# Post-norm decoder layer on one core: the splitting of the expert weights moved among steps 36 to 62

## What is computed

```python
x = _layernorm(x + _L0_attn_ref(x, ...))                    # state-space mixer: chunked scan, 4 heads of 64
x = _layernorm(x + _L0_xattn_ref(x, ctx_1024, ctx_1024, ...))  # cross attention: 16 heads of 8, 256 x 256 softmax
x = _layernorm(x + _L0_ffn_ref(x, ...))                     # 8 experts, the best 2 of each row
...
# experts (w0, w1: 8 x 128 x 512; wo: 8 x 512 x 128)
layer_1 = _gmm(sorted_hidden, w0, onehot)
layer_2 = _gmm(sorted_hidden, w1, onehot)
intermediate = jax.nn.silu(layer_1) * layer_2
layer_3 = _gmm(intermediate, wo, onehot)
```

## Time and profile before

| | |
|---|---|
| median of 3 runs | 422.5 us (418.44, 422.5, 1061.15) |
| the profiled execution | 415.8 us, its span 414.5 us |
| TensorE busy, granted clock | 349.5 us (84%), 0.98 of full speed |
| VectorE busy | 292.3 us (71%) |
| ScalarE busy | 235.2 us (57%) |
| GpSimd busy | 230.4 us (56%) |

### The profile page before, as it was taken

One profiled execution on the slowest core, in us unless ns is written; L12 is line 12 of the kernel. 1 busy time (PEld: TensorE's weight loads), 2 busy tenths in 40 slices (PEclk: granted clock), 3 DMA queues, 4 the chain that ended last, 5 costly groups with the idle time before them and its releaser, 6 DMA issues.

```text
span 414.5 us, 9020 instructions
## 1 busy us (share of the span) xinstructions
PE 349.5 (84%) x2869; PEld 238.0 (57%) x2869; DVE 292.3 (71%) x836; ACT 235.2 (57%) x460; POOL 230.4 (56%) x341
## 2 busy tenths in 40 slices
PE   1999977888988999988878899988997999999900
PEld 1666645556544545444444445567776899898800
DVE  3555645888788888878796736376776877877737
ACT  2677644432667666455577687744644665666514
POOL 2660598855354435271569788546575445445525
PEclk9999999999999999999999999999999999999975
DMA  8933322636515040322624343211112211111054
GB/s 269 336 110 106 87 85 77 187 94 186 171 33 166 5 140 5 99 70 75 196 69 131 117 155 102 74 32 40 53 41 78 78 53 40 53 52 35 32 171 146
DMA packets 44461, 41.97 MB, mean 101 GB/s; under 512 B 4560, under 2 KB 38416, under 8 KB 44416
## 3 DMA queue, kind: packets, MB, share of 16 engines
q1 hardware_dynamic: 41136, 35.10, 28.1%
q0 software_dynamic: 2272, 4.69, 3.2%
q10 hardware_dynamic: 1008, 1.61, 1.1%
HBM read 26.36 MB, written 14.75 MB: 99 GB/s over the span
## 4 chain that ended last, share of the span: by engine, by line
PE 56%; DVE 20%; issue 7%; POOL 7%; ACT 4%; another core or an unknown queue 3%; DMA 2%; ACTq 0%; DVEq 0%; POOLq 0%
PE banks L1017 12%; DVE nm L1210 8%; PE banks L1044 6%; PE banks L1032 4%; PE banks L859 4%; PE banks L698 4%; PE banks L907 3%; PE banks L1045 2%; PE banks L755 2%; PE banks L937 2%; PE banks L763 2%; DVE ctx_in L1152 2%; PE banks L806 2%; PE banks L934 1%
## 5 line engine op out<-in xcount | busy, mean ns | idle before, releaser
L1210 DVE TENSOR_REDUCE nm<-banks 128x4 f32<-128x1024 f32 x64 | 78.1, 1220 | 17.5 <-PE banks L850 11.4
L1520 ACT ACTIVATE probs_all<-banks 128x1024 f32<-128x1024 f32 x64 | 65.4, 1023 | 36.0 <-PE banks L859 29.6
L1017 PE MATMUL banks<-w_split,scores_in 128*128 x234 | 64.5, 410 | 0.0
L1342 DVE TENSOR_TENSOR ctx_in<-ctx_in,banks 128x512 f32<-128x512 f32 x39 | 26.8, 687 | 27.3 <-ACT ctx_in L1567 21.4
L1017 PEld LDWEIGHTS banks<-w_split,scores_in 128*128 128x128 f32 x234 | 40.8, 189 | 7.7 <-issue 0.9
L1705 POOL DMA_INDIRECT slots_dram<-rows,place_u x32 | 31.9, 996 | 23.5 <-DVE count L1302 16.1
L1727 POOL DMA_INDIRECT y_dram<-x,scatter_u x39 | 38.5, 987 | 11.4 <-POOL x L1723 9.7
L1567 ACT ACTIVATE ctx_in<-banks 128x512 f32<-128x512 f32 x39 | 23.3, 599 | 36.7 <-PE banks L1017 31.9
L859 PE MATMUL banks<-scores_in 32*128 32x256 f32 x256 | 32.2, 326 | 12.0 <-ACT probs_all L1520 6.0
L1044 PE MATMUL banks<-w_split,scores_in 128*128 x156 | 39.1, 327 | 2.8 <-ACT scores_in L1573 2.1
L907 PE MATMUL banks<-probs_all,vals 128*9 128x256 f32 x512 | 39.7, 381 | 0.2
(11 more groups left out here) (230 smaller groups left out, 802.2 us busy)
## 6 DMA issues: line engine op xcount, KB each, us to landing
scores_in<-k_dram SPq DMA_DIRECT2D x32, 128.0 KB, 2.7
scores_in<-q_dram SPq DMA_DIRECT2D x32, 128.0 KB, 2.7
ctx_in<-in_L_ffn_w SPq DMA_DIRECT2D x16, 256.0 KB, 2.7
cs_wide<-cs_dram SPq DMA_DIRECT2D x14, 256.0 KB, 3.7
scores_in<-slots_dram SPq DMA_DIRECT2D x39, 65.0 KB, 1.9
k_dram<-split_qk SPq DMA_DIRECT2D x8, 256.0 KB, 2.5
q_dram<-split_qk SPq DMA_DIRECT2D x8, 256.0 KB, 2.3
ctx_in<-in_L_ffn_wo SPq DMA_DIRECT2D x8, 256.0 KB, 2.9
```

The source lines that it names most:

```text
L1017: m = TE.matmul(up_bank(i, j), xT[:, i % XT, xh, :], all_weights[:, c + j * FF:][:, bass.ds(expert_at[i], FF)], start=n == 0, stop=n == 2)
L1210: V.tensor_reduce(most, maxima_of(n).rearrange("p (j k q) -> p j k q", j=2, k=TPS), AX_X, ALU.max, negate=True).then_inc(s["nmax"], 1)
L1520: C.activation(probs(n).rearrange("p j k q -> p (j k q)"), EXPS, ACT.Exp, scale=SCALE).then_inc(s["probs"], 1)
```

## The change

One line of constants is new, and three lines of `middle_order` use it:

```diff
 LAST_MIXER = tile_step(NT - 1) + LAGS[0][1]
+WEIGHTS_FROM, WEIGHTS_OMITTED = LAST_MIXER + 2, (40, 41, 49)
...
-        if n == LAST_MIXER + 4:
+        if n == WEIGHTS_FROM:
             for i in range(W_RING):
                 yield "load_weights", i
-        elif n >= LAST_MIXER + 6 and piece < PIECES:
+        elif n >= WEIGHTS_FROM + 2 and n not in WEIGHTS_OMITTED and piece < PIECES:
             yield "split_weights", piece
             if W_RING <= piece + 2 < PIECES:
                 yield "load_weights", piece + 2
```

## The result

The changed kernel takes 421.11 us in the median of 20 runs (419.2 to 428.43), the kernel before 419.72 us over 20 runs on the same chip. The ratio is 1.0039, with a 95% interval of 1.0022 to 1.0057: slower by 0.9 to 2.4 us, far inside 2%. Ratios here leave out executions more than 1.5% above the fastest of their kernel, while medians in us are over all executions. The sum in the prediction was +0.6 us, and the loss of the medians, 1.4 us, is over twice that. The time of 421.11 us is 1.6 us above the forecast 419.5 us and inside the range of 415 to 424 us. The profiled execution took 420.03 us (span 418.6) against 415.8 us (span 414.5).

What follows compares the result with a forecast made beforehand. A TensorE-ScalarE cycle was taken to set the pace in steps 33 to 51, TensorE from 52. +0.52 - 0.28 + 0.35 = +0.6 us on a mean of 418.9 gave 419.5 us, range 415 to 424 us.

Steps and rivals of the forecast that it cites:

- (a): Steps 36 to 38: the split put into step 37 delays ScalarE's next exponential and the delay is carried on, +0.52 us.
- (b): Steps 41 and 49: gains of the omitted splits are lost in waits tied to GpSimd's scatters; 0, bounds 0 and -0.52 each.
- the omissions pay: Rival: the waits of steps 43 and 51 aren't tied to the scatters, gains are kept; sum -0.45 us, chance 0.25.
- (c): Step 44: piece 6's load comes earlier, so its 0.42 us wait for weights goes; -0.28 us.
- (d): Steps 50 to 61: the same splits one step later, with TensorE the bound and exponentials having time to spare; 0.
- (e): Step 62, tail: the last piece on GpSimd holds VectorE's normalization, delaying TensorE's transposes; +0.35 us, bounds 0 and 0.6.
- The collision: Rival, step 43: GpSimd's piece 5 starts before VectorE's `chosen` and holds it; 0.7 to 2.0 us let through, chance 0.15.

Runs made afterwards that it cites:

- set A: Batches on one chip where the kernel before takes 418.6 to 420.0 us and ScalarE waits in step 43.
- set B: Batches on one chip where the kernel before takes 411.8 us and the wait in step 43 is absent.
- choice_first: The changed kernel, but GpSimd's piece 5 waits until VectorE's `chosen` is done; 421.53 us, 1.0028 of before.
- scatter_late_again: The kernel before with GpSimd's scatters of one tile moved from step 40 to step 44, on set A; 423.92 us in one run.
- last_ahead: The changed kernel, but the last piece is split at the start of step 62, ahead of the variance; 422.26 us, 1.0055 of before.
- after_again: The changed kernel itself, unedited, on set B; 411.63 us, 0.9995 of before.
- before_again: The kernel before, unedited, for a second profile, on set B; 411.95 us.
- all_three: Changed kernel omitting step 37 instead of 40, piece 5 held for the choice, last piece ahead of the variance; 409.89 us, 0.9963 of before on set B.
- omit37_again: The changed kernel with step 37 left out in place of 40, on set A; 428.18 us over 6 runs, 1.0114 of before.

## Why the prediction was wrong, step by step

**The time.** The sum of +0.6 us was added to a mean of 418.9 us, taken of three executions of the kernel before, so that the forecast of 419.5 us lay below the median of 422.5 us that was then known. Over 20 runs that median is 419.72 us, and the same sum would have given 420.3 us. That 421.11 us lies within the range of 415 to 424 us says little, since the range was made wide enough for single executions. The prediction also held that a change under 2% can hardly be told from none; 20 runs of each kernel told 0.4% from none.

**(a) Split of step 37: right in its row, incomplete as a whole.** +0.50 us at exponential 38, forecast +0.52. What the working left out is that the delay makes TensorE stand 0.73 us in place of 0.29, and that its clock then fell in every profile of set A. I had counted the delay as 0.5 us and nothing as following from it. On set B the same stand-still (0.76 us) was followed by a clock of 1.00 in three profiles of three, so it isn't a sufficient cause. In the profile of after the fall made exponential 42 some 1.5 us late (an estimate: +0.95 us between 38 and 42, where the omission of 41 should have given -0.52), and the wait of step 43 took nearly all of it back: at 43 it is +0.60 us, 0.10 above the delay alone. In choice_first it is +1.39 us there.

**(b) Omissions at 41 and 49: right for this chip, not for all.** Exponential 50 came 0.52 us earlier and 51 gave 0.54 back; scatter_late_again shows that the wait moves with the scatters. My direct comparison was of the right rows. By the Trainium skill (SBUF — State Buffer, Who interferes with whom) PE and ACT never wait on anyone for ports; the row `229.07 ... [1.72 <-remote]` shows ScalarE waiting until 0.87 us after GpSimd's last scatter. Whether it is a port that it waits for no row says, and VectorE's like wait speaks as well for a cause on TensorE's side. On set B, where the wait is absent, the rival "the omissions pay" holds for the most part: 0.52 us were kept at 41 and 0.32 us at 49.

**(c) Weights of piece 6: right.** No DMA wait before the split of step 44, and 44 to 45 falls to 1.71 us from 1.99. Of this 0.28 us the first profile keeps little, since 43 to 44 grew by 0.26 us beside it. On set B it is worth 0.83 us.

**(d) Steps 52 to 61: right.** From +1.64 at 51 to +1.65 us at 58 and +1.47 us at 61.

**(e) The tail: right in mechanism and in size.** The normalization took 1.54 us (forecast 1.3 to 1.6). From exponential 63 to the first expert copy it is 3.86 us against 3.49: +0.37 us, forecast +0.35 with bounds of 0 and 0.6. last_ahead, which takes only this away, has 3.49 again; on set B the normalization costs 0.53 us (after_again against before_again). The row at 63.99, where both parts took 1.20 us behind GpSimd, was the nearer one in kind: there too GpSimd goes straight from `rs` into its next product. What the forecast hadn't is the +0.48 us between 62 and 63. It stands ahead of the normalization, choice_first with the same late piece has 0.21 us of it, and its cause is open.

**The collision: the step that failed.** It was a rival with a chance of 0.15 and stood at nothing in the sum, though its two starts were only 0.01 us apart in the working; it should have had half. It happened as described, with piece 5 ahead by 0.09 us, and let 1.04 us through, inside the 0.7 to 2.0 us given. choice_first, which holds piece 5 behind `chosen`, takes 0.85 us of it away (45 to 46 2.41 us, before 2.22). In last_ahead it hit `choice`, and after_again has `choice` held for 1.33 us (`221.92`). The start of `chosen` had been compared with that of piece 5 alone; `choice`, 0.3 us ahead of it, is as open to it.

So the term that was left at zero (the collision, +1.0 us) and the unexplained 0.48 us ahead of exponential 63 carry the trace from the forecast +0.6 us to what it shows, +1.8 us against the second and +2.3 us against the first profile of before, the median of the runs being +1.4 us. What the clock adds to this median isn't separated. After has 15 of 20 executions under 0.972, with a median of 421.1 us, and the other five have 420.8 us; the kernel before has, in two other batches of set A, 419.4 us for those above and 421.0 us for those below. Where the clock held, after is then 1.4 us slower, about as much as the collision and the held normalization make, but five executions beside another batch are few. The kernels with both waits mended should have shown a gain and did not within their intervals; why is open.

## What to carry to other kernels

Where two engines take turns and hold each other's pace, look not only at the length of a split or a copy put in between but also at the stand-still that it gives TensorE, and compare the granted clock of many executions, not of one profile. Where two instructions on VectorE and GpSimd come within a tenth of a microsecond of each other in the working, book the collision as an even chance and hold one behind the other. A gain that is made ahead of a wait tied to something else makes that wait longer, and can cost more than it gave: what was best on one set of runs (all_three, 0.9963) was worse than before on the other (1.0065). Of the versions that ran on both sets none beats the kernel before on both.

## What the runs showed of the hardware

- After a stand-still of TensorE of 0.73 us behind an otherwise busy stretch, its granted clock fell to 0.50 for 3 to 7 us in six profiles of six on set A. After one of 0.76 us at the same place it stayed at 1.00 in three profiles of three on set B. Once, in omit37_again, it stayed at 0.50 for 43 us with TensorE busy throughout.
- The same program differed by 2% between batches on different chips (419.7 and 411.8 us), and not by a factor. On the one side exponential 27 follows 26 after 3.9 to 4.1 us and 35 follows 34 after 3.8 to 4.0 us, on the other both after 1.7 us; and from the first expert copy to the end it is 145.1 to 147.8 us on one side and 142.0 to 142.4 us on the other.
- GpSimd's 1.27 us splits held VectorE's `chosen` (0.17 us) for 1.21 and its normalization (0.60 us) for 1.54. The Trainium skill (SBUF — State Buffer, Who interferes with whom) says that a VectorE instruction with two SBUF inputs contends with a GpSimd one that reads SBUF, and for `chosen`, which has two such inputs, the trace agrees.
